# Macaron transformer block: inverse roots of four tiles in the stage before, and transposes taken tile by tile

## The reference

```python
def _layernorm(x, axis=-1, eps=1e-05):
    m = jnp.mean(x, axis=axis, keepdims=True)
    v = jnp.var(x, axis=axis, keepdims=True)
    return (x - m) / jnp.sqrt(v + eps)

x = x + 0.5 * _L0_ffn_ref(_layernorm(x, axis=-1), ...)
x = x + _L0_attn_ref(_layernorm(x, axis=-1), ...)
x = x + 0.5 * _L0_ffn_ref(_layernorm(x, axis=-1), ...)
x = x + 0.5 * _L1_ffn_ref(_layernorm(x, axis=-1), ...)
x = x + _L1_attn_ref(_layernorm(x, axis=-1), ...)
x = x + 0.5 * _L1_ffn_ref(_layernorm(x, axis=-1), ...)
return x
```

## Time and profile before

| | us |
|---|---|
| median of 3 runs | 1725.32 |
| lowest and highest | 1724.57, 1725.44 |
| the profiled execution's own time | 1734.16 |
| its span | 1732.30 |
| mean granted TensorE clock of the span | 0.97 |
| busy: PE, PEld, DVE, ACT, POOL | 1603.9, 1248.4, 1001.3, 914.6, 990.0 |

### The profile page before, as it was taken

The page is one execution under the profiler, slowest core; times in us unless marked ns, Lnnn a source line. Parts: engine busy times, 40 slices in busy tenths (PEclk is TensorE's granted clock), DMA queues, the critical chain, the costliest instruction groups (busy, mean ns, idle before and its releaser), DMA issues. The chain is left out here.

```text
span 1732.3 us, 26681 instructions
## 1 busy us (share of the span) xinstructions
PE 1603.9 (93%) x8364; PEld 1248.4 (72%) x8364; DVE 1001.3 (58%) x2614; ACT 914.6 (53%) x1881; POOL 990.0 (57%) x1156
## 2 busy tenths in 40 slices
PE   6899999998979996889999999999999999979998
PEld 4587565656667874678878787877878788767886
DVE  6651656644583237465665666666675756666235
ACT  2212767661232222677777777777777777731231
POOL 2342646530313632688777788778787787812533
PEclk9899989998989998999999999999999999989999
DMA  2200000001076643445344443534445344454934
GB/s 88 104 1 3 2 1 2 2 2 38 1 271 220 226 151 115 91 104 122 86 110 111 107 115 79 124 94 109 121 100 131 73 104 91 92 184 161 344 126 152
DMA packets 311297, 179.99 MB, mean 104 GB/s; under 512 B 281608, under 2 KB 282968, under 8 KB 308769
## 3 DMA queue, kind: packets, MB, share of 16 engines
q1 hardware_dynamic: 299360, 152.54, 31.4%
q0 software_dynamic: 11840, 26.25, 4.8%
HBM read 111.08 MB, written 22.54 MB: 77 GB/s over the span
## 5 line engine op out<-in xcount | busy, mean ns | idle before, releaser
L1381 POOL TENSOR_TENSOR st_prob<-st_prob,st_rinv 128x512 f32<-128x512 f32 x256 | 273.7, 1069 | 167.4 <-DVE st_rinv L1463 167.4
L1385 POOL TENSOR_TENSOR st_plane<-st_prob,st_plane 128x512 f16<-128x512 f32 x256 | 311.1, 1226 | 0.2
L1470 DVE TENSOR_REDUCE st_nmax<-st_score 128x1 f32<-128x512 f32 x256 | 175.3, 685 | 198.1 <-PE st_score L114 197.6
L1316 ACT ACTIVATE st_prob<-st_score,st_nmax 128x512 f32<-128x512 f32 x256 | 175.3, 685 | 82.2 <-DVE st_nmax L1470 80.3
L1300 ACT ACTIVATE st_plane<-st_prob 128x512 f16<-128x512 f32 x256 | 160.3, 626 | 108.1 <-POOL st_prob L1381 107.9
L1426 DVE CAST st_ptlo<-st_plane_t 128x512 fp32r<-128x512 f16 x256 | 175.2, 685 | 2.4 <-DMA st_plane_t<-st_plane 2.4
L1295 ACT ACTIVATE st_pthi<-st_plane_t 128x512 fp32r<-128x512 f16 x256 | 159.7, 624 | 6.8 <-DMA st_plane_t<-st_plane 6.6
L2143 DVE CUSTOM_DVE_ANT_0 st1b_dump<-st1b_score,st1b_maskrow 128x128 f32<-128x128 f32 (+3 forms) x256 | 112.8, 488 | 82.2 <-PE st1b_score L1796 56.5
L791 POOL DMA_INDIRECT st_xg<-rows,st_source x62 | 62.8, 1013 | 108.3 <-DVE st_source L979 61.3
L1992 ACT ACTIVATE st1b_slabs<-st1b_across 128x512 f32<-128x512 f32 (+1 forms) x192 | 91.1, 531 | 61.0 <-PE st1b_across L1818 45.8
L661 PE MATMUL st_bank<-st_xts,st_raw 128*128 128x128 f32 x992 | 121.0, 275 | 0.7 <-issue 0.7
(11 more groups left out here) (395 smaller groups left out, 4001.4 us busy)
## 6 DMA issues: line engine op xcount, KB each, us to landing
st_raw<-in_moe_w SPq DMA_DIRECT2D x40, 768.0 KB, 17.8
sorted_outs<-st_ln_xn SPq DMA_DIRECT2D x62, 256.0 KB
st_qraw<-in_gqa_q SPq DMA_DIRECT2D x8, 1024.0 KB, 5.2
st_oraw<-in_gqa_o SPq DMA_DIRECT2D x8, 1024.0 KB, 5.2
rows<-st_ln_xn SPq DMA_DIRECT2D x2, 2048.0 KB, 14.7
st_kvraw<-in_gqa_kv SPq DMA_DIRECT2D x8, 512.0 KB, 3.9
st_plane_t<-st_plane SPq DMA_TRANSPOSE x256
st1a_raw<-in_w_attn SPq DMA_DIRECT2D x3, 1024.0 KB, 5.5
```

Of the source, the lines that this page charges most:

```text
L1316: act.activation(prob[:, t, :], score[t][:, :], ACT.Exp, bias=nmax[:, slot:slot + 1], accum_out=rsum[:, slot:slot + 1]).then_inc(exp_ready, 1)
L1381: pool.tensor_tensor(prob[:, t, :], prob[:, t, :], rinv[:, slot:slot + 1].broadcast_to([P, T]), ALU.mult).then_inc(norm_ready, 1)
L1385: pool.tensor_tensor(plane[t][:, T:2 * T], prob[:, t, :], plane[t][:, 0:T], ALU.subtract).then_inc(lower_ready, 1)
L1470: dve.tensor_reduce(nmax[:, slot:slot + 1], score[t][:, :], AX, ALU.max, negate=True).then_inc(nmax_ready, 1)
```

## The change

The four inverse roots of tiles 0 to 3 are worked out in the making stage, once their moments are there (`early` on VectorE, `early_root` on ScalarE); the buffers for variances and roots move from the stage to the whole kernel. The reading stage writes rows 0 to 3 without waiting, then works out the four other roots, then writes rows 4 to 7. `close` aggregates only tiles 4 to 7. TensorE turns a tile as soon as its row is there, into four banks at once. In the LiME stage the early part stands ahead of the last tile's addition; in the experts' stage all four moments of tiles 0 to 3 and the early part stand ahead of the first of the last four additions; in the grouped attention stage `root_table` and `early_root` move ahead of the last `out_hi`; at the start of the kernel the early part follows the moments of the fourth tile.

```diff
+def inverse_root(dve, root, cols, step, done):
+    ve, ra, rb, rc = (root[n][:, cols] for n in ("ve", "ra", "rb", "rc"))
+    dve.reciprocal(ra, root["sd"][:, cols]).then_inc(step, 1)
+    dve.wait_ge(step, done + 1)
+    dve.tensor_tensor(rb, ra, ra, ALU.mult).then_inc(step, 1)
+    dve.wait_ge(step, done + 2)
+    dve.tensor_tensor(rc, rb, ve, ALU.mult).then_inc(step, 1)
+    dve.wait_ge(step, done + 3)
+    dve.tensor_scalar(rb, rc, -0.5, 1.5, ALU.mult, ALU.add).then_inc(step, 1)
+    dve.wait_ge(step, done + 4)
+    dve.tensor_tensor(rc, ra, rb, ALU.mult).then_inc(step, 1)
+    dve.wait_ge(step, done + 5)
...
 class Moments:
...
-    def close(self, dve):
+    def early(self, dve, taken):
+        half = slice(0, TB)
+        dve.wait_ge(self.stats_ready, taken)
+        for t in range(TB):
+            dve.bn_aggr(self.mv[:, t, :], self.stats[:, t, :]).then_inc(self.mv_step, 1)
+        dve.wait_ge(self.mv_step, TB)
+        dve.tensor_scalar(self.root["ve"][:, half], self.mv[:, half, 1], 1e-5, None, ALU.add).then_inc(self.mv_step, 1)
+        dve.wait_ge(self.early_std, 1)
+        inverse_root(dve, self.root, half, self.mv_step, TB + 1)
+
+    def early_root(self, act):
+        act.wait_ge(self.mv_step, TB + 1)
+        act.activation(self.root["sd"][:, 0:TB], self.root["ve"][:, 0:TB], ACT.Sqrt).then_inc(self.early_std, 1)
+
+    def close(self, dve, rest):
         dve.wait_ge(self.stats_ready, NT)
-        for t in range(NT):
-            dve.bn_aggr(self.mv[:, t, :], self.stats[:, t, :]).then_inc(self.mv_ready, 1)
-        dve.wait_ge(self.mv_ready, NT)
+        for t in rest:
+            dve.bn_aggr(self.mv[:, t, :], self.stats[:, t, :]).then_inc(self.mv_step, 1)
+        dve.wait_ge(self.mv_step, NT + 6)
...
 class Norm:
...
     def vector_rows(self, dve):
...
+        dve.tensor_scalar(self.root["ve"][:, late], self.mv[:, late, 1], 1e-5, None, ALU.add).then_inc(self.var_ready, 1)
+        for t in range(self.early):
+            row(t)
         dve.wait_ge(self.std_ready, 1)
...
+        inverse_root(dve, self.root, late, self.rstd_step, 0)
+        for t in range(self.early, NT):
+            row(t)
...
     def tensor(self, pe):
-        for n, (h, k) in enumerate(self.order):
-            pe.wait_ge(self.xn_ready, TB * (h + 1))
+        for h in range(B):
             for t in range(TB):
-                last = pe.transpose(self.bank[n][:, t * P:(t + 1) * P], self.rows[h * TB + t][:, k * P:(k + 1) * P], self.ident[:, :])
-            last.then_inc(self.turned_ready, 1)
+                pe.wait_ge(self.xn_ready, TB * h + t + 1)
+                for k in range(KC):
+                    last = pe.transpose(self.bank[h * KC + k][:, t * P:(t + 1) * P], self.rows[h * TB + t][:, k * P:(k + 1) * P], self.ident[:, :])
+                    if t == TB - 1:
+                        last.then_inc(self.turned_ready, 1)
...
 # lime_ffn_stage, scalar
                     act.wait_ge(ident_loaded, 16)
                     entry.root_table(act)
+                    entry.early_root(act)
                 norm.scalar_std(act)
...
                 moments.root_table(act)
+                moments.early_root(act)
...
 # lime_ffn_stage, vector
                         entry.take(dve, t)
-                    entry.close(dve)
+                        if t == TB - 1:
+                            entry.early(dve, TB)
+                    entry.close(dve, range(TB, NT))
...
                 for j in range(NT):
+                    if j == NT - 1:
+                        dve.wait_ge(x_added, j)
+                        moments.take(dve, order[j - 1])
+                        moments.early(dve, j)
                     dve.wait_ge(tile_ready, j + 1)
...
-                    if j >= 1:
+                    if 1 <= j < NT - 1:
                         dve.wait_ge(x_added, j)
                         moments.take(dve, order[j - 1])
...
 # moe_stage, vector
-                for t in range(TB):
-                    add_step(NI - 1, 1)
+                if not last_stage:
+                    for t in range(TB):
+                        wait(dve, *written[t])
+                        moments.take(dve, t)
+                    moments.early(dve, TB)
+                add_step(NI - 1, 1)
+                for t in range(TB, NT):
+                    if t + 1 < NT:
+                        add_step(NI - 1, 1)
                     if not last_stage:
                         wait(dve, *written[t])
                         moments.take(dve, t)
...
 # gqa_stage, scalar
                     turned_hi(LAST, NU - 1, t)
+                moments.root_table(act)
+                moments.early_root(act)
                 out_hi(LAST, NU - 1)
-                moments.root_table(act)
...
 # gqa_stage, vector
                     moments.take(dve, t)
+                moments.early(dve, TB)
                 out_lo(LAST, NU - 1)
...
 # heads_block, vector
                     moments.take(dve, t)
+                moments.early(dve, TB)
                 for t in range(TB, NT):
...
 # macaron_kernel
+        env["root"] = {n: s.sb(n, [P, NT]) for n in ("ve", "ra", "rb", "rc")}
+        env["root"]["sd"] = env["table"][:, NT:2 * NT]
```

More of the change, by code:

```diff
@@ L157, in __init__ @@
             rows = [self.xn[:, t, :] for t in range(NT)]
-        self.ve, self.sd = s.sb("ln_ve", [P, NT]), s.sb("ln_sd", [P, NT])
-        self.ra, self.rb, self.rc = s.sb("ln_ra", [P, NT]), s.sb("ln_rb", [P, NT]), s.sb("ln_rc", [P, NT])
+        self.root, self.early = env["root"], early
         self.rows = rows
@@ L166, in vector_rows, with row @@
     def vector_rows(self, dve):
-        x, mv, ve, ra, rb, rc = self.x, self.mv, self.ve, self.ra, self.rb, self.rc
-        dve.tensor_scalar(ve[:, :], mv[:, :, 1], 1e-5, None, ALU.add).then_inc(self.var_ready, 1)
-        dve.wait_ge(self.std_ready, 1)
-        dve.reciprocal(ra[:, :], self.sd[:, :]).then_inc(self.rstd_step, 1)
-        dve.wait_ge(self.rstd_step, 1)
-        dve.tensor_tensor(rb[:, :], ra[:, :], ra[:, :], ALU.mult).then_inc(self.rstd_step, 1)
-        dve.wait_ge(self.rstd_step, 2)
-        dve.tensor_tensor(rc[:, :], rb[:, :], ve[:, :], ALU.mult).then_inc(self.rstd_step, 1)
-        dve.wait_ge(self.rstd_step, 3)
-        dve.tensor_scalar(rb[:, :], rc[:, :], -0.5, 1.5, ALU.mult, ALU.add).then_inc(self.rstd_step, 1)
-        dve.wait_ge(self.rstd_step, 4)
-        dve.tensor_tensor(rc[:, :], ra[:, :], rb[:, :], ALU.mult).then_inc(self.rstd_step, 1)
-        dve.wait_ge(self.rstd_step, 5)
-        for t in range(NT):
-            dve.tensor_scalar(self.rows[t], x[:, t, :], mv[:, t, 0:1], rc[:, t:t + 1], ALU.subtract, ALU.mult).then_inc(self.xn_ready, 1)
+        late = slice(self.early, NT)
+        def row(t):
+            dve.tensor_scalar(self.rows[t], self.x[:, t, :], self.mv[:, t, 0:1], self.root["rc"][:, t:t + 1],
+                              ALU.subtract, ALU.mult).then_inc(self.xn_ready, 1)
+        dve.tensor_scalar(self.root["ve"][:, late], self.mv[:, late, 1], 1e-5, None, ALU.add).then_inc(self.var_ready, 1)
+        for t in range(self.early):
+            row(t)
+        dve.wait_ge(self.std_ready, 1)
+        inverse_root(dve, self.root, late, self.rstd_step, 0)
+        for t in range(self.early, NT):
+            row(t)
     def vector_lo(self, dve):
@@ L190, in scalar_std @@
         act.wait_ge(self.var_ready, 1)
-        act.activation(self.sd[:, :], self.ve[:, :], ACT.Sqrt).then_inc(self.std_ready, 1)
+        act.activation(self.root["sd"][:, self.early:NT], self.root["ve"][:, self.early:NT], ACT.Sqrt).then_inc(self.std_ready, 1)
     def scalar_hi(self, act):
@@ L448, in _ @@
                 moments.take(dve, order[NT - 1])
-                moments.close(dve)
+                moments.close(dve, range(TB, NT))
 def moe_stage(nc, env, dram, name):
@@ L1018, in _ @@
                 if not last_stage:
-                    for t in range(TB, NT):
-                        wait(dve, *written[t])
-                        moments.take(dve, t)
-                    moments.close(dve)
+                    moments.close(dve, range(TB, NT))
 def gqa_stage(nc, env, dram, name):
```

15 lines of the change are left out of this document (10 added, 5 removed).

## The result

| | median | lowest to highest | runs |
|---|---|---|---|
| kernel before, beside it on the same chip | 1725.32 us | 1714.22 to 1728.27 | 11 |
| changed kernel | 1737.36 us | 1728.26 to 1741.89 | 11 |

The ratio is 1.0069, 95% interval 1.0047 to 1.0092: 12 us slower. The forecast was 1730.0 with a range up to 1733.5, so the sign was right and the size wrong. The profiled execution took 1739.89 us with a span of 1738.2; that span is only 5.9 us over the one before.

A forecast was written before the change was run, and what follows sets the result against it. TensorE, busy 93% of the span, was taken to bound the kernel, so only its standstills at the start and stage handovers could pay. 2.9 - 1.3 + 1.9 - 0.6 + 1.8 = +4.7 us on 1725.32 gave 1730.0, range 1724.5 to 1733.5.

The forecast's parts named there:

- All four rivals: Clock doesn't bite (1727.0, 0.22); start escapes GpSimd (1722.8, 0.10); transposes leave clock alone (1728.6, 0.05); clock low everywhere (1733.5, 0.13).
- Start, +2.9: Kernel start: early root delays later moments, GpSimd's subtraction holds up rows, x-low begins later; +2.9 us, ends 2.2 and 3.6.
- Tail of stage four, +1.9: Stage four's end: four moments and early part delay the first add, TensorE stands 2.7 us; +1.9 us, ends 0.7 and 2.4.
- Other tails, -1.3: Ends of stages one, two, three and five: four aggregates go, 0.33, 0.32, 0.33 and 0.32 us gained; -1.3 us.
- Heads, -0.6: Stage starts: stage six gains 0.9 us, stage four loses 0.3, others 0; -0.6 us, ends -1.5 and +0.6.
- Clock, +1.8: Heads of stages two, four, five, six: TensorE idles longer, matmuls meet low clock; 0.4, 0.5, 0.5, 0.4 us, +1.8 in all.
- turning tile by tile, 0: Stage heads: as many transposes and copies, later filling of banks hidden by weight copies or x-low; 0 us.

The follow-up runs named there:

- p2: The whole changed kernel plus 123 idle instructions on ScalarE in stage four, against the kernel before: ratio 1.0036.
- p2b: The changed kernel with the same 123 idle ScalarE instructions once more, beside the kernel before on another chip: ratio 1.0039.
- p1: The kernel before plus five tiny ScalarE copies ahead of stage five, against the kernel before: 1736.13 against 1730.73 us, ratio 1.0031.
- t1: The kernel before with turning tile by tile and nothing else, against the kernel before: ratio 1.0005.
- e3: The changed kernel with turning bank by bank as before, early roots kept, against the kernel before: ratio 1.0074.
- e7: The changed kernel with stage one's start, stage four's tail and bank-by-bank turning as before, ScalarE's loop moved to 1043 instructions, against the kernel before: ratio 1.0011.
- filled kernels: Kernels with idle instructions added on ScalarE that move stage five's loop to a place where it doesn't stall.
- e3b: The changed kernel with turning bank by bank as before and 123 idle ScalarE instructions, against the kernel before: ratio 1.0025.
- e8: The changed kernel with only tiles 0 to 3 turned tile by tile, the rest bank by bank, loop at 1043 instructions, against the kernel before: ratio 1.0057.
- e9: As e8, with stage one's start and stage four's tail also as before, against the kernel before: ratio 1.0018.
- p4: The kernel before plus two small ScalarE copies ahead of stage five: 1726.66 us, one execution.

## Why the prediction was wrong

**The step that failed: a term that wasn't in the sum.** It set out "2.9 - 1.3 + 1.9 - 0.6 + 1.8 = +4.7 us". With the stall taken out, the change costs 0.37%, 6.5 us, and the 4.7 lies inside the intervals of both p2 and p2b. The 5.4 us or so on top come with the stall in ScalarE's loop in stage five, which begins five instructions later in the changed kernel (920 in the place of 915): one root in each of stages one to four and one more at the kernel's start. p1 shows it from one side and p2 from the other; the size is known within p1's 1.2 to 9.3 us only, and the traces show 3.3 us of it as waits of TensorE. The prediction counted what each moved instruction costs where it stands, and never what it does to the code behind it. All four rivals shared that gap, so the range did too.

**Start, +2.9: right in size and way.** Early reciprocal "near 10.3" came at 11.14, as the identity landed at 10.80 and not 9.83 in this execution; tile 7's moments end at 14.6 for 13.8; rows held up by GpSimd, x-low at 24.22 for 23.75. Over all traces +2.5 at the first product.

**Tail of stage four, +1.9: right.** TensorE idle 2.76 us for "2.7". From the end of the last combine, 669.76, to the end, 681.78, it takes 12.0 us, before 9.6: +2.4, the dear end. Over all traces the way up to stage five's first matmul grows by 2.5, and the order of the tail is 1.2 of it.

**Other tails, -1.3: too much.** In stage three from the add of the seventh tile to the end 5.74 us before and 5.59 after, -0.15 for -0.33; in stage five from the last split 7.38 and 7.13, -0.25 for -0.32. Rows, one execution each; these show two of the four:
```profile
478.98 0.68 DVE L480 SCALAR_TENSOR_TENSOR all_x<-st_bank,all_x 128x512 f32<-128x512 f32 x1
...
484.19 0.38 DVE L174 BATCH_NORM_AGGREGATE all_mv<-all_stats 128x2 f32<-128x6 f32 x4
...
1539.17 0.69 DVE L1474 TENSOR_TENSOR st_olo<-st_outp,st_ohi 128x512 fp32r<-128x512 f32 x1 [2.73 <-ACT st_ohi L1347]
...
1545.92 0.38 DVE L174 BATCH_NORM_AGGREGATE all_mv<-all_stats 128x2 f32<-128x6 f32 x4
```
**Heads, -0.6: too little.** Stage six gains 1.8 for 0.9: the first transpose came 3.7 us nearer, because four rows took 2.63 us and not the 0.97 each that I had carried over from a row under GpSimd's memsets. Stage four, where I had +0.3, gains 0.15. And the gain isn't the early roots' alone. From variance to first matmul, stage six takes 9.8 to 10.8 us in the five kernels with neither part of the change, 9.43 in t1, which has no early roots, and 9.1 to 9.5 in those with early roots and banks. VectorE and TensorE in t1:
```profile
1530.57 0.51 DVE L168 TENSOR_SCALAR st_ln_ve<-all_mv 128x8 f32<-128x8 f32 x1 [1.27 <-PEq L76]
```
```profile
1540.00 0.47 PE L112 MATMUL st_bank<-all_xhi,st_ghi 128*128 128x512 f32 x1 [0.84 <-DVE all_xlo L187]
```
So turning tile by tile, which I had put at 0, may by itself give most of this gain; t1 is one execution.

**Clock, +1.8, and turning tile by tile, 0: mis-sized, and wrongly parted.** The low clock at the first matmuls of stages two and five came as forecast, but in stage five it costs 1.4 us over the first 24 matmuls where I had 0.5, and there it comes with the order that I had priced at nothing: I asked only whether the order delays a copy, not what it does to TensorE's pauses. In stage two it isn't the order: the first matmul takes 0.80 us in e3 and e7, with banks, too. In medians the order is worth about 2.2 us in the filled kernels; by itself, without early rows, nothing that shows (t1). One reading was wrong, though its result holds: the x4 in the stretch at 77 counts the matmuls that touch this microsecond, not four starts. At the low clock p2b's start 0.42 us apart (690.24, 690.66), and it is this less 0.23 that makes the 0.2 us for each. I had set the Trainium skill's rule that transposes don't bring the clock up ("TensorE: Matmul & The Clock Gate", section on PE-mode transpose) against a row of before. The traces after side with the row: in e3b the clock rises from 0.50 to full while only transposes run (0.85 mean from 691 to 693, with the matmuls not before 695).

**What is open.** How the 6.5 us part exactly: e7's 1.9, 2.2 to 2.4 for start and tail (6.7 from e8 to e9), 2.2 for the order are differences of medians whose errors are as large. What besides idle time decides the clock at stage five's first matmul. And no kernel beat the one before: e7 is the best with early roots.

## What to carry to other kernels

A loop on an engine has a place in its instruction stream, and adding two to five instructions anywhere ahead of it can cost a stall at every jump back; so when a change costs more than its parts, compare the packets of the instruction queue and look for "issue" idle at the first instruction of the loop, and test it with the old kernel plus as many idle instructions. Work made early is a gain only where the reader stood waiting for it: at the start and in stage four's tail the same two microseconds stood ahead of something that was on the path. And what an engine does sooner it may pay with its clock later.

## What the runs showed of the hardware that I had not expected

The stall behind the jump back of ScalarE's loop (247 instructions) is 1.4 to 1.7 us an iteration (2.3 in p4) and goes with some 25 more packets of the instruction queue in five iterations, 8 KB each (0.20 MB). It comes with the loop 2, 4 or 5 instructions further on than in the kernel before, and not with 0, 64 or 128. The Trainium skill, "Runtime: NRT & Kernel Launch", section on instruction fetch mechanics, says that a taken branch whose target is no longer held forces a fetch before execution goes on. The trace agrees as to the stall; which places are dear, the section's block of 256 instructions doesn't tell: if the loop lies inside one block at 0 and crosses a border at 2, it crosses one at 64 and 128 too. What makes a place dear stays open.
